# A two-layer gated cross-attention block with experts: the first rows fetched in the dense blocks, roots ahead of the last pieces, two pieces made behind the experts, and another order in an attention prologue

## The reference, cut to what matters

```
x = x + tanh(g_xattn[0]) * attn0(layernorm(x), ctx, mask)       # 16 heads
x = x + tanh(g_ffn[0])   * (shared_swiglu + top 8 of 64 experts)(layernorm(x))
x = x + tanh(g_xattn[1]) * attn1(layernorm(x), ctx)             # no mask
h = layernorm(x)
x = x + tanh(g_ffn[1])   * (h + mlp(h) + top 2 of 8 gelu experts)(h)
```

## Time and profile before

| What | Value |
|---|---|
| median of three runs | 2265.39 us |
| profiled execution, its own time | 2262.2 us |
| its span | 2260.4 us |
| PE busy | 2117.3 us (94%) |
| DVE / ACT / POOL busy | 57% / 46% / 23% |
| mean granted clock of PE | 0.97 |

### The profile page before, as it was taken

One profiled execution on the slowest core, in us unless ns is written; L12 is line 12 of the kernel. 1 busy time (PEld: TensorE's weight loads), 2 busy tenths in 40 slices (PEclk: granted clock), 3 DMA queues, 4 the chain that ended last, 5 costly groups with the idle time before them and its releaser, 6 DMA issues. The chain is left out here.

```text
span 2260.4 us, 39527 instructions
## 1 busy us (share of the span) xinstructions
PE 2117.3 (94%) x13342; PEld 1498.7 (66%) x13343; DVE 1279.0 (57%) x2751; ACT 1028.9 (46%) x2379; POOL 516.5 (23%) x501
## 2 busy tenths in 40 slices
PE   6999999997997999999788999999889979999998
PEld 3777777775953444444367777777669437777775
DVE  4677777776672222222347777777640227777776
ACT  2466666665221111111215666666553005666655
POOL 3000000001453554555420000000014002223332
PEclk9999999997998999999989999999989989999999
DMA  5010000011143999998721000000122236655661
GB/s 183 28 33 33 33 31 21 20 72 66 38 191 119 337 320 337 343 332 258 213 81 53 28 28 28 28 28 2 76 101 59 49 123 255 257 210 209 231 223 22
DMA packets 63757, 288.19 MB, mean 127 GB/s; under 512 B 10627, under 2 KB 10797, under 8 KB 44293
## 3 DMA queue, kind: packets, MB, share of 16 engines
q1 hardware_dynamic: 43892, 247.41, 29.5%
q0 software_dynamic: 19728, 38.97, 7.9%
HBM read 259.82 MB, written 32.93 MB: 130 GB/s over the span
## 5 line engine op out<-in xcount | busy, mean ns | idle before, releaser
L776 ACT ACTIVATE probs<-ps,less_max 100x360 f32<-100x360 f32 (+1 forms) x384 | 212.3, 562 | 166.6 <-DVE less_max L606 88.6
L1647 PE MATMUL pgu<-ring,xT 128*128 x560 | 267.5, 601 | 5.4 <-issue 2.1
L762 ACT ACTIVATE pTs<-pt 128x300 f32<-128x300 f32 x512 | 189.9, 426 | 122.4 <-PE pt L485 121.3
L1647 PEld LDWEIGHTS pgu<-ring,xT 128*128 128x128 f32 x560 | 100.3, 192 | 112.9 <-issue 112.5
L485 PE MATMUL pt<-ident,probs 100*128 100x100 f32 (+1 forms) x1152 | 137.5, 257 | 32.1 <-ACT pTs L762 26.7
L485 PEld LDWEIGHTS pt<-ident,probs 100*128 100x128 f32 (+1 forms) x1152 | 116.2, 141 | 62.5 <-issue 36.1
L2021 DVE TENSOR_TENSOR ws_low<-w,ws_high 128x2048 fp32r<-128x2048 f32 x63 | 143.1, 2292 | 24.2 <-ACT ws_high L1952 24.2
L362 PE MATMUL pp<-first 128*128 128x512 f32 x564 | 143.0, 402 | 1.2 <-DVE first L386 1.2
L362 PE MATMUL po<-first 128*128 128x512 f32 (+1 forms) x564 | 142.1, 401 | 1.4 <-DVEq L664 1.4
L606 DVE CUSTOM_DVE_ANT_0 ps<-ps,madd 100x362 f32<-100x362 f32 (+1 forms) x256 | 128.7, 564 | 23.6 <-PE ps L471 23.4
L358 PE MATMUL po<-first 128*128 128x362 f32 (+1 forms) x720 | 137.7, 341 | 1.4 <-PEq L190 1.1
(11 more groups left out here) (324 smaller groups left out, 4301.0 us busy)
## 6 DMA issues: line engine op xcount, KB each, us to landing
ring<-in_l_ew SPq DMA_DIRECT2D x64, 1536.0 KB, 8.6
w<-in_l_ew SPq DMA_DIRECT2D x64, 1024.0 KB, 7.9
xnT<-in_ctxT SPq DMA_DIRECT2D x14, 1444.0 KB, 6.6
first<-in_l_up SPq DMA_DIRECT2D x2, 4096.0 KB, 13.5
b<-in_l_eb SPq DMA_DIRECT2D x8, 1024.0 KB, 4.7
wd<-in_l_down SPq DMA_DIRECT2D x2, 2048.0 KB, 8.0
xn_rows<-mid SPq DMA_DIRECT2D x16, 200.0 KB
moe<-moe_sum SPq DMA_DIRECT2D x16, 200.0 KB
```

Source lines behind the costliest of these rows:

```text
L762: act.activation(pTs[:, g % 2, j, 3 * half:3 * half + 3, :].rearrange("k c q -> k (c q)"), pt[:, half, 0:3 * S], ACT.Copy).then_inc(t_out, 1)
L776: act.activation(probs[g % 2 * HPC + j][:, k0:k1], ps[j][0:S, 0:k1 - k0], ACT.Exp, bias=less_max[:, g, seg, j:j + 1], scale=-1.0 if masked ...
L1647: last = pe.matmul(pgu[p][:, :], xT[p][:, c, :], wgu[c], start=c == 0, stop=c == DC - 1)
```

## The change

Joined: in both dense blocks POOL now does `first_rows`: it makes the index of the first tile (layer 0: of tiles 0 and 1) and issues the gather into buffers of its own, `xg_first`, once `token_ready` is there. The experts' PE reads these. SP's two waits at the end of the dense blocks go to POOL in the experts' block, ahead of its first adding scatter. So that the slots are ready earlier, layer 0 looks up tile 6 before the down product of tile 5 instead of 6, and layer 1 transposes its table before the last two down products.

Between the layers: PE makes the first two of the ten pieces at the end of the experts' block, into two banks that were free there, after a wait for the five splits (`ahead_low`). In the next block ACT takes the roots before it brings out the last two pieces, and DVE does the low parts of these keys after the scaling.

Prologue of attention 1: v5 moves behind the second group's scores and two transposes on PE, behind `normalised(0, 3)` on DVE; ACT moves one context split behind the next exponents.

```
@@ beside MADE_AHEAD
+EARLY = 2
@@ attention, ahead: PE
                     scores(0, 0, 1, 0)
+                    scores(0, 0, 1, 1)
+                    transposed(0, 0, 0, True)
+                    transposed(0, 0, 1)
                     first_piece("v", 5)
-                    transposed(0, 0, 0, True)
-                    scores(0, 0, 1, 1)
-                    transposed(0, 0, 1)
                     transposed(0, 0, 2)
@@ attention, ahead: DVE
                     normalised(0, 0)
-                    first_piece("v", 5)
-                    normalised(0, 1)
                     maxima(0, 0, 1, 1)
                     segments_apart(0, 1)
+                    normalised(0, 1)
                     normalised(0, 2)
                     normalised(0, 3)
+                    first_piece("v", 5)
@@ attention, ahead: ACT
                     turned(0, 0, 0)
-                    next_high(1, 0)
                     exponents(0, 1, 1, range(HPC), True)
                     shares(0, 1)
                     turned(0, 0, 1)
+                    next_high(1, 0)
@@ dense_and_route: SP, at its end
-                sp.wait_ge(sum_begun, 16 * G)
-                sp.wait_ge(x_out, 16 * B)
                 sp.wait_ge(env.rows_out, 16 * B)
@@ dense_and_route: POOL
+                def first_rows(p):
+                    pool.tensor_copy(env.index_first[p][:, :], env.slot_token[:, p:p + 1]).then_inc(index_ready, 1)
+                    pool.wait_ge(index_ready, p + 1)
+                    pool.sem_inc(passed, 1)
+                    pool.indirect_dma_start(out=env.xg_first[p][:, :], in_=env.xn_rows[:, :], ...)
                 if swiglu:
+                    pool.wait_ge(slots_ready, 1)
+                    for p in range(2):
+                        pool.memset(env.xg_first[p][:, :], 0.0).then_inc(x_clear, 1)
                     for t in range(G):
                         with_weights(t)
+                    (waits: x_clear 2, rows_out, token_ready 1)
+                    for p in range(2):
+                        first_rows(p)
...
+                if not swiglu:
+                    (waits: rows_out, token_ready 1)
+                    first_rows(0)
@@ dense_and_route: PE
-                        if swiglu and t > 0:
-                            look_up_slots(t - 1)
-                        if swiglu and t == G - 1:
-                            look_up_slots(t)
+                        if not swiglu and n == NDH * G - 2:
+                            (wait table_in, two transposes of the table, then_inc table_mm)
+                        for looked_up in {1: (0,), 2: (1,), 3: (2, 3), 4: (4,), 5: (5, 6)}.get(t, ()) if swiglu else ():
+                            look_up_slots(looked_up)
@@ dense_and_route: ACT, after the output of tile t
-                        if t + 2 < G:
-                            with_token(t + 2)
+                        for later in {0: (2,), 1: (3,), 2: (4, 5), 3: (6,)}.get(t, ()):
+                            with_token(later)
@@ dense_and_route: DVE; layer 1 at n == NDH * G - 1, ahead of the wait for its product
+                            dve.wait_ge(table_mm, 1)
+                            (copies of slot_token, then_inc token_ready, and of slot_weight)
@@ experts_swiglu: POOL
-                for p in range(2):
-                    fetch(p, p)
-                for p in range(2):
-                    fetch_next(1, p)
+                for p in range(2):
+                    fetch(2 + p, p)
+                (waits: sum_begun 16 * G, x_out 16 * B)
@@ experts_swiglu: PE, behind the last expert
+                pe.wait_ge(ahead_low, len(SPLIT) + 1)
+                for n in range(EARLY):
+                    piece_ahead(pe, env, MADE_AHEAD[n], env.early_banks[n])
@@ experts_gelu: POOL
-                fetch(0)
                 fetch_next(1)
+                (wait: sum_begun 16 * G)
@@ combine_and_normalise: ACT
+                def roots():
+                    act.wait_ge(var_done, B + 1)
+                    act.activation(std[:, :], stats[:, :, 0], ACT.Sqrt).then_inc(std_done, 1)
                 for i, what in enumerate(MADE_AHEAD):
+                    if i == len(MADE_AHEAD) - 2:
+                        roots()
...
-                act.wait_ge(var_done, B + 1)
-                act.activation(std[:, :], stats[:, :, 0], ACT.Sqrt).then_inc(std_done, 1)
@@ combine_and_normalise: DVE
-                keys_low(6)
-                keys_low(7)
...
                 for t in range(B): (scaling of the rows)
+                keys_low(6)
+                keys_low(7)
```

More of the change, by code:

```diff
@@ L55, with piece_ahead @@
               ("k", 3, 0), ("k", 3, 1))
+EARLY = 2
+def piece_ahead(pe, env, what, bank):
+    wk, wv, ctx = env.wide_first[0:2], env.wide_first[2:4], env.mid_first
+    for c in range(DC):
+        for n, m in PARTS:
+            first, last_one = c == 0 and (n, m) == PARTS[0], c == DC - 1 and (n, m) == PARTS[-1]
+            if what[0] == "k":
+                g, (k0, k1) = what[1], SEG[what[2]]
+                last = pe.matmul(bank[:, 0:k1 - k0], wk[n][:, c, g * P:(g + 1) * P], ctx[m][:, c, k0:k1],
+                                 start=first, stop=last_one)
+            else:
+                kc = what[1]
+                last = pe.matmul(bank[:, :], ctx[n][:, c, kc * P:(kc + 1) * P], wv[m][:, c, :],
+                                 start=first, stop=last_one)
+    return last
 class Env:
@@ L926, in dense_and_route @@
         if swiglu:
-            at_tile = env.after_xnT + before_it([P, K, 3, NS])
+            with ExitStack() as later:
+                second, *env.xg_first = [later.enter_context(nc.sbuf_tensor(env.name("after"), s, dt)) for s, dt in (
+                    ([P, K, 3, NS], F32R), ([P, D], F32), ([P, D], F32))]
+            at_tile = env.after_xnT + [second]
         eq = sb("eq", [P, G, K, E])
@@ L1195, in _ @@
                         n = hf * G + t
-                        if swiglu and t > 0:
-                            look_up_slots(t - 1)
-                        if swiglu and t == G - 1:
-                            look_up_slots(t)
+                        if not swiglu and n == NDH * G - 2:
+                            pe.wait_ge(table_in, 16)
+                            for a in range(2):
+                                last = pe.transpose(turned_table[:, a, :], table[:, :, a], env.ident[0:NS, 0:NS])
+                            last.then_inc(table_mm, 1)
+                        for looked_up in {1: (0,), 2: (1,), 3: (2, 3), 4: (4,), 5: (5, 6)}.get(t, ()) if swiglu else ():
+                            look_up_slots(looked_up)
                         if n >= 2:
@@ L1205, in _ @@
                         last.then_inc(down_mm, 1)
-                if not swiglu:
-                    pe.wait_ge(table_in, 16)
-                    for n in range(2):
-                        last = pe.transpose(turned_table[:, n, :], table[:, :, n], env.ident[0:NS, 0:NS])
-                    last.then_inc(table_mm, 1)
             @block.scalar
@@ L1510, in experts_swiglu @@
         ring_in, w_ready = env.ring_in, sem("w_ready")
-        x_in = [sem(f"x_in{p}") for p in range(2)]
+        x_in = env.x_in
         added, sum_at_ready = [sem(f"added{p}") for p in range(2)], sem("sum_at_ready")
@@ L1517, in experts_swiglu @@
         raw_in, rest_in = [sem(f"raw_in{n}") for n in range(3)], sem("rest_in")
-        ctx_high, w_high = sem("ctx_high"), sem("w_high")
+        ctx_high, w_high, ahead_low = sem("ctx_high"), sem("w_high"), sem("ahead_low")
+        env.early_banks = [pb(f"pk{n}", [P, 512]) for n in range(EARLY)]
         def last_pair_of(engine):
@@ L2098, in combine_and_normalise @@
         NB = 4
-        pk = [cx.enter_context(nc.psum_tensor(env.name(f"pk{n}"), [P, 512], F32)) for n in range(NB)]
+        pk = env.early_banks + [cx.enter_context(nc.psum_tensor(env.name(f"pk{n}"), [P, 512], F32))
+                                for n in range(EARLY, NB)]
         pT = [cx.enter_context(nc.psum_tensor(env.name(f"pT{n}"), [P, DC, S], F32)) for n in range(2)]
@@ L2118, in _ @@
             def _(pe):
-                for i, what in enumerate(MADE_AHEAD):
+                for i, what in enumerate(MADE_AHEAD[EARLY:], EARLY):
                     if i >= NB:
@@ L2123, in _ @@
                         pe.wait_ge(*((k_out, K_AHEAD.index(read) + 1) if read[0] == "k" else (v_out, V_AHEAD.index(read) + 1)))
-                    for c in range(DC):
-                        for n, m in PARTS:
-                            first, last_one = c == 0 and (n, m) == PARTS[0], c == DC - 1 and (n, m) == PARTS[-1]
-                            if what[0] == "k":
-                                g, (k0, k1) = what[1], SEG[what[2]]
-                                last = pe.matmul(bank_of(what)[:, 0:k1 - k0], wk[n][:, c, g * P:(g + 1) * P],
-                                                 ctx[m][:, c, k0:k1], start=first, stop=last_one)
-                            else:
```

(9 more changed lines are left out.)

65 lines of the change are left out of this document (46 added, 19 removed).

## The result

The kernel after runs in 2255.94 us (median of 6 runs, 2250.91 to 2258.41), the kernel before, beside it, in 2266.57 (6 runs, 2262.94 to 2273.3). Ratio 0.995, 95% interval 0.9931 to 0.9968: some 10.6 us faster, and just at the 0.5% that can be told from no change. The profiled execution of the kernel after takes 2255.86 us, its span 2254.1, so the two profiles differ by only 6.3. A later set of 8 runs of the same kernel gave 2253.87 (2245.98 to 2259.69), ratio 0.9953 (0.9936 to 0.9969), and its profiled execution has a span of 2244.2. One profile is thus worth some 5 us either way; what follows leans on stretches and on what the same stretch did in several runs.

The account below looks back on a forecast made before the run. PE, busy 94% of the span, was taken to bound the kernel, with its stops between blocks and the clock falls after them; 7.2+3.3+3.2-1.2 = 12.5 us gained, time 2253, own range 2247 to 2260, stated range 2242 to 2264.

Parts of the forecast that it names:

- Join of layer 0: From dense block 0 to its experts: earlier gathers let PE start sooner, 7.2 us gained, between 1 and 10.
- Join of layer 1: From dense block 1 to its experts: no wait for rows, the bias then limits; 3.3 us gained, between 0.8 and 4.2.
- Pieces and roots: Between the layers: two pieces made early, roots wait only for the statistics; transposes 3.2 us earlier, bounds 0 and 6.
- Prologue: Prologue of attention 1: moving v5 leaves longer PE gaps; 1.2 us lost, between 3 gained and 3 lost.
- The drain did not take the joins: Rival at both joins: POOL's drain comes a full 9.6 us after late gathers; 3.8 us gained, time 2261.6, chance 0.21.
- no drain behind a gather is near 20 us: Slower rival: a drain needs about 20 us from a gather's issue, both joins lose; 15 us slower, 2280, chance 0.05.
- all covered and the clock up: Rival: drain unseen, no clock fall at first join or between layers, prologue gains 1; 20.9 us, time 2244.5, chance 0.22.
- theory B: For e6, last down product to first transposes between the layers: table load costs its drain too, 38.5 us or more.

Follow-up runs that it names:

- e3: Kernel after with the look-ups of dense block 0 on PE at their old places: 2250.5 us, ratio 0.9946 to the kernel before.
- e9: Kernel after with e1, e3, e8 and e10 together: 2235.41 us, ratio 0.9865 to the kernel before.
- e11: e9 with DVE writing the slot numbers ahead of the counts of tiles in dense block 0: 2234.19 us, ratio 0.9869 to the kernel before.
- e10: Kernel after with SP loading the rows for the sums ahead of the second half of the down weights in dense block 1: 2242.67 us, ratio 0.9905.
- e2: Kernel before with only the new order of the prologue of attention 1: 2268.84 us, ratio 1.0024 to the kernel before.
- e8: Kernel after with an expert's whole bias one place earlier in SP's queue, ahead of the fourth part of the weights: 2254.22 us, ratio 0.9951.
- e5: Kernel after with no piece made behind the experts (`EARLY = 0` for 2): 2248.54 us, ratio 0.9934 to the kernel before.
- e12: e11 with no piece made behind the experts (`EARLY = 0`): 2235.4 us, ratio 0.9864 to the kernel before.
- e1: Kernel after with the prologue of attention 1 in its old order on PE, DVE and ACT: 2246.75 us, ratio 0.9933 to the kernel before.
- e6: Kernel after with the roots at their old place on ACT, behind all outputs of pieces: 2255.27 us, ratio 0.9961 to the kernel before.
- e4: Kernel after with a quarter of the first expert's bias loaded right behind the first part of the weights: 2252.44 us, ratio 0.995.

## Why the prediction was right, and where its terms were off

The forecast was 2253 for 2255.94 and 2253.87, by a sum of 12.5 us for 10.6 and 11.8 of medians. The mechanism was the one forecast, joins closed up to the next thing that is late and a loss in the prologue. Its terms fit less well than their sum: measured in the first trace of the kernel after they are 4.85, 2.8, 6.2 and -3.8, 10.1 together. One is 3.0 too small and two are 2.4 and 2.6 too large, so that the sum came close is in part luck.

- *Join of layer 0, 7.2 predicted, 4.85 measured* (at the third `px`). Failed: "the look-ups of tiles 3 and 6 may wait for POOL's weights, up to 1 us in all". They waited 3.0. Two tables of DVE ran beside POOL at 2.66 instead of 1.11, 3.1 together, and POOL waited for each; the slots came 2.5 earlier and not 4, the bound that the text had for just this. In e3, with the old places, tables of 1.12 and no wait are back. "I bound it by 0 and 9.6 and take 7" was the other miss: the drain ends 2.7 to 2.9 behind the second gather's issue, below all three rows, and did not bind. Had the look-ups not held PE up, it would have (e3, e9, e11). Two of the three rows could not stand for a gather: at 1121.80 and 2252.73 the program itself waits for its scatter to land, 4.7 and 4.8 us, and only then come drains of 4.07 and 2.60. The third stands behind a queue of scatters and ends at 1765.1, when the last of them has landed (1764.5). And "the gather is the shorter instruction" gave no reason for the 7: the scatter of the third row is shorter still (0.95) and has the longest distance (9.6). Of the clock 1.5 was counted; from the first to the third `px` it is 12.0 instead of 13.6, which is this 1.5.
- *Join of layer 1, 3.3 predicted, 2.8 measured* (F; 25.5 to 25.7 in six of the seven runs with that code, 24.06 in e10; before 28.4, 29.4 in e2). The mechanism is the one predicted, the bias (14.8 us to landing); e8 shows it. The first `ph`, for which the 3.3 was worked out, even gained 4.4; 1.6 went back to a fall of the clock behind the wait, which the text did not count. The 1.1 more come from the start of the block: POOL's drain ended 4.1 behind its gather and not 7, ahead of DVE's (1843.3 and 1844.8), so the first weights were issued 2.3 us behind DVE's last sum instead of 3.5. That is 1.2 earlier, where 0.3 had been put.
- *Pieces and roots, 3.2 predicted, 6.2 measured* at the query projection, 4.2 to 7.1 over the nine kernels with both. Failed: "combine starts at 1135.2, 2.7 later than today". It starts no later: PE waits for the first four of five splits, not for DVE's "last split", so the pieces end 0.2 before POOL's drain. The roots, put at 19.2 behind the block's start, follow at 19.7, and the table load, of which half was counted as saved, is saved whole. The bank waits cost 0.6. What the text did not see is that the pieces' part is gone again by the first `v2` (e5, e12), in e12 by the clock.
- *Prologue, -1.2 predicted, -3.8 measured* (D; -2.6 to -3.8 in nine runs, e1 and e2 alone for the cause). That is outside the term's own bounds of 3 gained and 3 lost. The idle times were right, 3.04 and 1.80 for 2.8 and 2.3, and 1.0 more in all, as the text had it. Failed: "it falls somewhere in the new order too", priced at nothing: it falls on v5, which costs 2.1, and on the transposes about it.
- *The rivals.* The drain did not take the joins, and no drain behind a gather is near 20 us (4.4 is the longest). Of the case with all covered and the clock up, the second run of the kernel after has the time (2245.98 us) and one part, no fall between the layers (C 3.8 shorter). The clock still falls at its first join, and its prologue loses 2.6. So a single run can have that rival's time without its mechanism.

The Trainium skill's 1.38 us of drain beside the load ("ScalarE: Activation LUTs", section "What ACT_TABLE_LOAD costs") does not show here either: in e6 the root stands at 1148.33, 0.02 behind the load of 1.28, and the output before the load ends at 1147.01, 0.02 ahead of it. By its rule e6 would have had theory B's 38.5 in B; it has 36.69, so the measurement decides against it in this place.

## What to carry to other kernels

Price a stop of PE by what runs behind it, not only by its length: in this prologue a fall over small, waiting matmuls cost little, one over twelve matmuls of 512 columns put 2.1 us onto their 2.99. When an edit takes a wait away, look in the trace for what lies within a few us behind it (here ACT, then POOL's drain, then the bias), for that is all it can gain. And read the queue to memory in the order in which data is needed: the largest gain of a single experiment was seven loads put ahead of one of 2 MB that PE first used 52 us after its issue (e10, 1733.98 and 1785.71).

## What the runs showed of the hardware

- POOL's drain at a block's end is over 2.7 to 2.9 us behind the start of the last gather's issue in layer 0, where two gathers are issued, and 3.9 to 4.2 in layer 1, where it is one (twelve profiles each). It ends 0.1 to 0.7 us behind the landing where the trace has that: 2.8 and 2.7 in layer 0 of e12, 4.1 and 3.4 in layer 1. The 7.5 and 9.0 behind scatters in the earlier trace rows hold a wait of the program for the landing, 4.8 and 4.7. Why a drain that starts behind a landed scatter still takes 2.6 and 4.1 was not tried.
- The load of ACT's table does not wait for the semaphore of the instruction that needs it: 1144.23, when the statistics came at 1148.37.
- With a load of 256 KB ahead of it that repeats one row of 2 KB in all 128 partitions, the next 1 MB of weights was there 11.4 us behind the first issue (e4), against 7.5 to 9.4 without. At the 413 to 426 GB/s of that stretch (windows of the kernel after, 1850 to 1862) 256 KB would take some 0.6, an estimate. One run, and no row length but this was tried.
- The same code took 403.5 to 410.3 us in the loop of experts 0, and single executions of the kernel after lie between 2246.0 and 2259.7: a single profile's end says nothing of 5 us, its stretches do.
